# Another order of work in the first 40 microseconds of a fused Mamba and FFN kernel, on all engines

## The reference, cut to what matters

```python
x = x + 0.5 * ffn(layernorm(x))        # quantised weights, LoRA, bias
x = x + attn(layernorm(x))             # rmsnorm, Mamba-2, rmsnorm, gated MLP, both with residuals
x = x + 0.5 * ffn(layernorm(x))

# ffn:  W = (q - zeros) * scales        (groups of 64 inputs share a scale and a zero)
#       y = x @ W.T + (1/16) * (x @ lora_A.T) @ lora_B.T + bias
# mamba2: z, xs, B, C, dt = split(h @ w_in.T); xBC = silu(conv4(xs|B|C) + conv_b)
#         dt = softplus(dt + dt_bias); chunked scan with cumulative decay; y * silu(z); @ w_out.T
```

## Time and profile before

| | us |
|---|---|
| median of 3 runs (lowest to highest) | 752.79 (752.75 to 752.86) |
| the profiled execution, its own time | 752.77 |
| its span in the profile | 751.0 |
| TensorE, VectorE, ScalarE, GpSimd busy | 736.6, 639.3, 455.9, 341.7 |
| mean granted TensorE clock | 0.998 of 2.4 GHz |

### The profile page before, as it was taken

How to read it: one execution, slowest core, us unless ns; L and a number is a source line. 1 busy time by engine, 2 the same in 40 slices (tenths; PEclk the granted TensorE clock), 3 DMA queues, 4 the chain that set the end, 5 groups by cost and what they waited for, 6 DMA issues and landing times.

```text
span 751.0 us, 10693 instructions
## 1 busy us (share of the span) xinstructions
PE 736.6 (98%) x3443; PEld 361.7 (48%) x3443; DVE 639.3 (85%) x1254; ACT 455.9 (61%) x895; POOL 341.7 (46%) x393
## 2 busy tenths in 40 slices
PE   8999999999999999979999999999999999999998
PEld 4454455555555565434444444444444444444444
DVE  7899999889989997868999977977977978767994
ACT  4977888687787776444546456456356456444441
POOL 5731546565443458696423243243242242214574
PEclk9999999999999999999999999999999999999999
DMA  8934645575431233330612735634734733434465
GB/s 300 216 76 86 160 100 118 127 132 103 91 84 43 44 79 94 81 98 1 156 27 49 163 56 97 157 57 84 169 57 84 160 66 71 84 71 80 117 169 141
DMA packets 98886, 77.83 MB, mean 104 GB/s; under 512 B 65616, under 2 KB 73104, under 8 KB 98832
## 3 DMA queue, kind: packets, MB, share of 16 engines
q0 software_dynamic: 17280, 31.46, 23.7%
q1 hardware_dynamic: 78640, 41.09, 21.3%
q10 hardware_dynamic: 2912, 4.61, 2.0%
HBM read 24.94 MB, written 5.54 MB: 41 GB/s over the span
## 4 chain that ended last, share of the span: by engine, by line
PE 71%; DVE 16%; POOL 5%; issue 3%; ACT 3%; DMA 2%; SPq 0%; POOLq 0%; ACTq 0%; DVEq 0%
PE PS L2283 60%; DVE stage L1671 2%; PE PS L2429 1%; DMA x_t<-hb 1%; DVE st L1494 1%; PE PS L2421 1%; PE PS L2387 1%; PE PS L2414 1%; PE PS L2418 1%; PE PS L2397 1%; DVE raw L1671 1%; PE PS L2405 1%; PE PS L2379 1%; PE PS L2525 1%; DVE S L1628 1%
## 5 line engine op out<-in xcount | busy, mean ns | idle before, releaser
L2283 PE MATMUL PS<-h,w_in 128*128 128x512 f16 (+1 forms) x504 | 108.1, 369 | 0.0
L2283 PE MATMUL PS<-h,x_t 128*128 128x512 f16 x408 | 95.5, 383 | 0.0
L784 POOL DMA_DIRECT2D xs<-x x42 | 36.7, 881 | 91.5 <-ACT x L1361 90.7
L2283 PEld LDWEIGHTS PS<-h,w_in 128*128 128x128 f16 x504 | 48.8, 98 | 59.9 <-issue 11.0
L2283 PE MATMUL PS<-n_T,stage 128*128 128x512 f16 x288 | 71.9, 380 | 4.0 <-DVEq L1725 4.0
L1361 ACT ACTIVATE x<-PS,d_d 128x512 f32<-128x512 f32 x59 | 40.2, 682 | 39.1 <-PE PS L2283 36.8
L2283 PEld LDWEIGHTS PS<-h,x_t 128*128 128x128 f16 x408 | 39.7, 99 | 49.4 <-issue 4.5
L584 POOL TENSOR_TENSOR r<-mv,mhalf 128x1 f32<-128x1 f32 (+1 forms) x32 | 29.1, 910 | 50.4 <-DVE mv L1498 36.4
L1331 ACT ACTIVATE xds<-tm,dgh 128x512 f32<-128x512 f32 x24 | 17.3, 722 | 53.1 <-DVE tm L2204 53.1
L2283 PE MATMUL PS<-pre,stage 128*128 128x512 f16 x192 | 49.3, 379 | 0.0
L2283 PEld LDWEIGHTS PS<-n_T,stage 128*128 128x128 f16 x288 | 28.1, 98 | 38.3 <-DVEq L1725 4.5
(11 more groups left out here) (346 smaller groups left out, 1882.8 us busy)
## 6 DMA issues: line engine op xcount, KB each, us to landing
xs<-x POOLq DMA_DIRECT2D x58, 256.0 KB, 3.3
xs<-n POOLq DMA_DIRECT2D x21, 256.0 KB, 3.2
xl<-x POOLq DMA_DIRECT2D x17, 256.0 KB, 3.3
x_t<-x_in SPq DMA_DIRECT2D x16, 256.0 KB, 3.9
x_t<-hb POOLq DMA_DIRECT2D x16, 256.0 KB, 4.4
out<-x_t SPq DMA_DIRECT2D x15, 256.0 KB, 2.3
raw_gu<-gate_t SPq DMA_DIRECT2D x7, 512.0 KB, 4.5
raw_gu<-up_t SPq DMA_DIRECT2D x7, 512.0 KB, 6.4
```

The lines of the kernel that those rows point to most:

```text
L784: po.dma_start(end_row(c), d_tmps[d % 3], accum_op=ALU.add).then_inc(s_acc[d % 3], 16)
L2283: ins = pe.matmul(out_, lhs(a, b, k), rhs(a, b, k), start=first and n == 0, stop=last and n == len(todo) - 1)
```

## The change

No computation is added or taken away. On each engine the calls of the opening stand in another order:

- SP: row 0 is issued first, `lora_b` moves to ScalarE's queue (third there, behind `lora_a` and `zeros`), the bias goes ahead of `q` 2 and 3, and `w_out` is issued after the fourth `t1`.
- GpSimd: `ln0(1)` stands behind the bias scaling and `xb(0)`.
- VectorE: `prep0(0)` ahead of `zero_rows`; `prep0(1)` behind `ffn_weight(1)`, `prep0(2)` behind `ffn_weight(3)`; `ffn_max` behind `x1_stats(0)`; scales and `w_in_lo(0)` ahead of rows 3 and 4. The scaling of the taps becomes a step of its own, `scale_taps`, in the prologue.
- ScalarE: `w_in_sum` earlier, the diagonals later (two groups behind `w_in_hi`, one in the prologue).
- TensorE: transposes and the turns of the maxima stand inside the float32 products, and `conv_taps(b)` waits for its own diagonals only.

```diff
@@ sync
+            load_x(0, 0)
             sp_.dma_start(sc[0:QUAD, :], scales_t).then_inc(s_la, 16)
-            sp_.dma_start(w_rows[QUAD:2 * QUAD, :], lora_b_t).then_inc(s_la, 16)
-            load_x(0, 0)
             load_q(0)
             load_x(1, 1)
             load_q(1)
+            sp_.dma_start(hb[:, :], bias.broadcast_to([P, DM])).then_inc(s_hb, 16)
             load_q(2)
             load_q(3)
-            sp_.dma_start(hb[:, :], bias.broadcast_to([P, DM])).then_inc(s_hb, 16)
...
-            sp_.dma_start(w_out[:, :, :], w_out_t.rearrange("(h p) n -> p h n", p=P)).then_inc(s_wout, 16)
...
             t1(3)
+            sp_.dma_start(w_out[:, :, :], w_out_t.rearrange("(h p) n -> p h n", p=P)).then_inc(s_wout, 16)
@@ gpsimd
-            ln0(1, 1)
             po.wait_ge(s_hb, 16)
             chain(po.tensor_scalar(hb[:, :], hb[:, :], 0.5, None, ALU.mult))
             xb(0, 0)
+            ln0(1, 1)
@@ scalar, prologue
                 hi1(4, 0)
+                build_dw(2)
...
                 hi0(7, 3)
+                ac.wait_ge(e_small, 2)
                 conv(0, 3)
@@ scalar, opening
+            ac.dma_start(sel_rows[QUAD:2 * QUAD, :], lora_a).then_inc(s_la, 16)
             ac.dma_start(zt[0:QUAD, :], zeros_t).then_inc(s_la, 16)
-            ac.dma_start(sel_rows[QUAD:2 * QUAD, :], lora_a).then_inc(s_la, 16)
+            ac.dma_start(w_rows[QUAD:2 * QUAD, :], lora_b_t).then_inc(s_la, 16)
...
             hi0(1, 1)
-            tc0(1)
             ac.wait_ge(s_head, 48)
             ac.activation(a_neg[:, :], al[:, :], ACT.Exp).then_inc(e_aexp, 1)
-            ac.wait_ge(e_tab, 2)
-            build_dw(0)
+            w_in_sum(0)
+            tc0(1)
             hi0(2, 2)
-            build_dw(1)
-            build_dw(2)
+            w_in_sum(1)
             tc0(2)
-            w_in_sum(0)
             hi0(3, 3)
-            w_in_sum(1)
+            w_in_sum(2)
+            hi1(0, 0)
             tc0(3)
-            hi1(0, 0)
-            w_in_sum(2)
             w_in_sum(3)
+            hi0(4, 0)
             hi1(1, 1)
-            hi0(4, 0)
             tc0(4)
             hi1(2, 2)
             hi0(5, 1)
-            hi1(3, 3)
             tc0(5)
             ac.wait_ge(e_scale, 1)
             w_in_hi(W_IN_PIECES[0])
+            hi1(3, 3)
             w_in_hi(W_IN_PIECES[1])
+            build_dw(0)
+            build_dw(1)
@@ vector, small_scales and prologue
-                ve.wait_ge(e_dw, NPC)
-                chain(ve.tensor_scalar(cw[:, :, :], cw[:, :, :], d_ih[:, :], None, ALU.mult))
...
+            def scale_taps():
+                ve.wait_ge(e_dw, NPC)
+                chain(ve.tensor_scalar(cw[:, :, :], cw[:, :, :], d_ih[:, :], None, ALU.mult))
+                ve.sem_inc(e_small, 1)
...
                 lo0(6, 2)
+                scale_taps()
@@ vector, opening
+            prep0(0, 0)
             zero_rows()
-            prep0(0, 0)
             ffn_weight(0)
+            ffn_weight(1)
             prep0(1, 1)
-            ffn_weight(1)
-            prep0(2, 2)
             ffn_weight(2)
             ffn_weight(3)
+            prep0(2, 2)
             prep0(3, 3)
+            x1_stats(0, 0, B_P[0])
             ffn_max()
-            x1_stats(0, 0, B_P[0])
+            x1_stats(1, 1, B_P[1])
             max_row(0)
-            x1_stats(1, 1, B_P[1])
             lo1(0, 0)
             prep0(4, 0)
+            w_in_bound()
             x1_stats(2, 2, B_P[0])
-            w_in_bound()
             lo1(1, 1)
+            max_row(1)
             prep0(5, 1)
-            max_row(1)
+            both_scales()
             x1_stats(3, 3, B_P[1])
-            both_scales()
             lo1(2, 2)
+            w_in_lo(0)
             lo1(3, 3)
             x1_stats(4, 0, B_P[0])
-            w_in_lo(0)
             small_scales()
@@ tensor
             def conv_taps(b):
-                if b == 0:
-                    pe.wait_ge(e_dw, NPC)
+                pe.wait_ge(e_dw, b + 1)
...
+            def first_f(c, k0, k1):
...
+                for k in range(k0, k1):
...
             first_t0(0)
             ffn_parts(2)
             ffn_parts(3)
+            first_f(0, 0, 2)
             first_t0(1)
-            first_f(0)
+            first_f(0, 2, KB)
+            first_f(1, 0, 2)
             first_t0(2)
-            first_f(1)
+            first_f(1, 2, KB)
+            first_f(2, 0, 2)
+            first_t0(3)
             max_turn(0)
-            first_t0(3)
-            first_f(2)
+            first_f(2, 2, KB)
             max_spread(0)
-            first_f(3)
+            first_f(3, 0, 2)
+            first_t0(4)
+            first_f(3, 2, 3)
             max_turn(1)
-            first_t0(4)
+            first_f(3, 3, KB)
+            first_f(4, 0, 1)
             max_spread(1)
-            first_f(4)
+            first_f(4, 1, 2)
             first_t0(5)
-            first_f(5)
+            first_f(4, 2, KB)
+            first_f(5, 0, KB)
```

More of the change, by code:

```diff
@@ L2516, in first_t0 @@
                 last.then_inc(e_n0_tr, 1)
-            def first_f(c):
-                pe.wait_ge(e_n0T, c + 1)
-                if c - 1 > 0:
-                    pe.wait_ge(e_x1, c - 1)
-                for k in range(KB):
+            def first_f(c, k0, k1):
+                if k0 == 0:
+                    pe.wait_ge(e_n0T, c + 1)
+                    if c - 1 > 0:
+                        pe.wait_ge(e_x1, c - 1)
+                for k in range(k0, k1):
                     if c == 0:
@@ L2525, in first_f @@
                     last = pe.matmul(bank(B_P[c % 2]), nT32[c % 2][:, k, :], wf[:, k, :], start=k == 0, stop=k == KB - 1)
-                last.then_inc(e_ffn, 1)
+                if k1 == KB:
+                    last.then_inc(e_ffn, 1)
             def max_turn(n):
```

## The result

The changed kernel takes 756.91 us (median of 6 runs, 756.58 to 757.23), the kernel before it 752.86 on the same chip (6 runs, 752.75 to 753.09): a ratio of 1.0054, 95% interval 1.0041 to 1.0067. That is 3.9 above the forecast of 753.0 and outside both ranges given (751.8 to 754.2, and 750.9 to 755.0 for 8 in 10). The execution profiled here took 756.58 itself, with a span of 754.8.

What follows compares the result with a forecast made beforehand. VectorE's chain was taken as the new bound: the projection's second half moves by +0.1 us and S costs another 0.1, so 752.77 plus 0.2 gives 753.0 us. Own range 751.8 to 754.2; for 8 in 10, 750.9 to 755.0.

Steps and rivals of the forecast that it cites:

- Row 0: VectorE's addition of the bias to row 0 was forecast at 17.1 instead of 19.63, 2.5 us earlier.
- bias landed at 8.7: Bias transfer on SP's queue: landing taken as 8.7 us, between an early bound of 7.7 and a late bound of 9.2.
- `xb(0)` 6.5: Transfer adding the bias to row 0: issued at 10.5, taken as 6.5 us long, landing at 17.0.
- `ffn_max` behind row 0: On VectorE, 3.0 us of `ffn_max` now follow row 0; with 1.8 for row 0, row 1 comes at 21.9.
- after 23: Sign that the forecast is wrong: VectorE adds row 1 before 20.5 or after 23.
- the waits of the fifth and sixth transposes: New TensorE gaps before the fifth and sixth rows' transposes: 0.6 to 1.2 and 0.3 to 0.8, together taken as 1.5 us.
- the fourth row's transpose holding the projection's second half: On TensorE, the projection's second half could start at 41.3 and waits 0.3 us more, until 41.6.
- The sum for TensorE itself: TensorE's opening: start 4.7, plus 32.46 of work, plus 1.5 of gaps, so the first projection starts at 38.7.
- the slow rival: Bias transfers decide: bias at 9.2, `xb(0)` and `xb(1)` taking 7.1 and 7.2, 754.9 us, if `xb(1)` lands after 21.3; chance 0.23.
- The first product: TensorE's first product, behind `lora_b`: forecast at 4.7, bounds 4.2 and 5.2, costing 0.5 us.
- does not do what it says: Rival: queues interleave, row 0 lands at 4.9, first product 5.2, bias unmoved, 753.6 us; chance 0.06, part of "same".
- `ln0(1)` behind the bias: On GpSimd, `ln0(1)` behind the bias scaling makes `hi0(1)` end near 12.5 instead of 11.5, before TensorE's need at 13.9: no cost.

Runs made afterwards that it cites:

- e1: The changed kernel with 12 instead of 7 junk products ahead of TensorE's first real product: 756.81 us.
- e2: The changed kernel with the bias issued third on SP's queue, ahead of all q and of row 1: 755.10 us.
- e3: The changed kernel with both edits, 12 junk products and the bias third on SP's queue: 754.36 us.
- e18: The kernel before with only the taps' diagonals and their scaling late, TensorE's taps waiting for each diagonal by itself: 753.18 us, ratio 0.9996 to 1.0017.
- e17: e13 with ScalarE's `hi1(3)` moved one step further, ahead of the fifth transposed copy `tc0(5)`: 753.86 us.
- e10: e6 with TensorE's opening put back to the order of before, VectorE keeping the changed order: 758.07 us.
- e12: The changed kernel with the early loads, VectorE's opening and TensorE's opening put back as before: 761.68 us.
- e15: e3 with `ffn_max` put back ahead of row 0 on VectorE: 754.42 us.
- e6: The changed kernel with SP's and ScalarE's early loads as before (`w_out` still late) and `zero_rows` ahead of `prep0(0)` on VectorE: 755.71 us.
- e9: e6 with `ffn_max` put back ahead of row 0 on VectorE: 754.24 us.
- e5: The kernel before with the change's order of loads and nothing else of it: 754.99 us.
- e7: The changed kernel with only VectorE's opening put back to the order of before: 758.96 us.
- e14: e9 with row 3's `hi1(3)` and `lo1(3)` moved ahead of the projection's weights on ScalarE and VectorE: 757.33 us.
- e13: e12 with GpSimd's `ln0(1)` ahead of its wait for the bias and ScalarE's `hi1(3)` ahead of the first `w_in` piece: 756.80 us.
- e4: The changed kernel with the early loads of SP and ScalarE in the order of before, `w_out` still late: 756.01 us.

## Why the forecast was wrong, point by point

**Row 0 was the step that failed**, in two of its three terms: bias landed at 8.7 (10.85 measured, +2.15) and `xb(0)` 6.5 (7.63, +1.1); the 1.8 on GpSimd held (1.82). The sum said 17.1, the chip 20.54. That 3.4 is nearly all of the 3.9. Put 17.1 into the relation above and S comes at 17.1 + 69.74 = 86.84, 0.35 later than before, against the 0.2 of the forecast. So all that follows row 0 in the sum was right to some tenths: `ffn_max` behind row 0 (+4.8 to row 1, measured 4.76; row 1 came at 25.30 for 21.9, beyond the sign "after 23"), the waits of the fifth and sixth transposes (0.6 to 1.2 and 0.3 to 0.8; 1.17 and 0.50), the fourth row's transpose holding the projection's second half by 0.3 (0.27). The sum for TensorE itself, 4.7 + 32.46 + 1.5, came out as 5.51 + 34.56 + 1.67. Its 2.1 of longer work is the half rate of the opening, but that is not what made the projection late: e1 ran at the full rate and started it 0.15 earlier.

**The bias's landing** was scaled with its place in SP's queue. Issued 1.42 sooner, with q2 and q3 behind it, it took 1.7 longer and landed later than before; the "late bound" of 9.2 had no room for a longer transfer. In e2, three places earlier, it took 4.3, so the place counts, but not by the bytes ahead of it alone. I had even written the slow rival with the right transfers, the bias at 9.2 and `xb` at 7.1, and gave it 0.23; its sizes were too small (10.85 and 7.63) and with them its 754.9. Its other condition, a late `xb(1)`, did not decide: row 1 had no idle time ahead of it at 25.30.

**The first product** was put at 4.7 with a late bound of 5.2, it came at 5.51: lora_b took 3.7 and not the 2.6 that it had taken at the front of its queue. The rival "does not do what it says" named this interleaving for row 0, which did land early (3.9 forecast; issued at 0.79, taken 3.2). The small inputs paid. The section "Issuing engines are not separate DMA queues" of the page "DMA: Bandwidth & Descriptors" of the Trainium skill fits that: moving lora_b to another engine's queue gave it no path of its own.

**The half rate was not in the forecast at all.** The trace of before had no idle time between junk and first product, so I read the junk as a fixed cost and not as something that sets the rate of what follows. With the start 0.8 late it put the first transposes at 11.55, not at 8.2. By itself it cost nothing (e1), since the bias was later still; once the bias is early it is worth 0.7 (e2 to e3), although lora_b landed 0.7 later in e3's profile. So a bias in time would not have brought row 0 to 17.1 either: TensorE's product held it at 19.18 in e2 and at 18.03 in e3.

**Right as forecast:** the late diagonals cost nothing that could be measured (e18). For the late output weights no run stands alone; e17 bounds them, with the rest that it keeps, by 0.9. **Wrong on GpSimd:** I had costed `ln0(1)` behind the bias at nothing: "`hi0(1)` ends at about 12.5 instead of 11.5, while TensorE needs it at 13.9: nothing". It ended at 15.3 (e10, e12); 1.8 of these 2.8 are the bias, landed at 10.5 there and not at 8.7. The changed order on TensorE covers that, so it did not show in the changed kernel, where VectorE's statistics of row 1 held `ln0(1)` until 14.34; in e10 and e12 it cost 2.3 to 2.4.

Of the 3.79 at S the pair accounts for 2.20 (after to e3; 2.5 in the medians), the place of `ffn_max` for 0.27 on top (e3 to e15, where the medians show nothing; 1.66 where VectorE waits for row 0, e6 to e9), and 1.32 are left in e15. I read this rest as two things: row 3's place behind the scale, and a transpose of the fourth row that took 3.5 us there and 2.7 in the changed kernel. No run removed either alone, and the rest stays argued.

## What to carry to other kernels

A step that fills a wait is free only where it stands. Before moving it behind the thing that is waited for, compute the arrival time at which the new order breaks even (here 16.75 at best, from the 69.74 us behind it), and ask whether every transfer on that path can make it. When an order was changed on several engines at once, undoing one engine's part does not measure this part: it breaks covers that the other engines' orders rely on, and must be read wait by wait.

## What the runs showed of the hardware

**With few warm-up products and an idle time behind them the first real ones run at half rate, and the clock column may not show it.** Idle 1.09 behind seven junk products (after), 1.47 (e2), 1.42 (e5) and 1.73 (e7): the next two pairs took 1.7 to 1.9 each, the third 0.9 to 1.6. Idle 0.17 and 0.85 behind twelve (e1, e3), and none (e15): 0.96 to 0.97 for the first pair and 0.86 from then on. The junk of the changed kernel and of e1, then the first products of e14, which follow seven junk products without idle time:

```profile
1.24 3.17 PE L2511 MATMUL PS<-junk 128*128 128x512 bf16 x7 [1.24 <-DVE junk L1481]
```

```profile
1.24 4.38 PE L2511 MATMUL PS<-junk 128*128 128x512 bf16 x12 [1.24 <-DVE junk L1481]
```

```profile
4.20 1.91 PE L2295 MATMUL PS<-h 128*128 128x512 f32 x2
5.91 1.49 PE L2298 MATMUL PS<-h 128*128 128x512 f32 x2
```

Seven junk products took 0.45 each, the five more of e1 0.24 each (0.33 in e15): the seven ran at the lower rate, and the rate rose behind them. Without idle time behind seven the outcome differs by execution: the first pair took 0.86 in e6 and 1.01 in the kernel before, but 1.7 in e10, e14 and e18. The runs don't separate the number of junk products from the idle time, nor show what makes one execution's rate rise sooner.

In the running kernel waits of 1.09 before and 1.30 (e9) left the rate alone, as did 2.01 (e13) and 2.79 (e14) ahead of the projection; 2.28 (e12), 2.42 (e10), 2.61 (e4), 2.98 (e7) and 3.60 (e12) did not. The length of the idle time alone doesn't decide it. The by-stretch rows (stretch, us, busy times, clock, DMA share, GB/s) of the changed kernel, and then of e10 behind its wait:

```profile
5.50:10.60 5.10, 5.09 (x6) 2.18 (x7) 1.83 (x3) 0.81 (x1) 1.14 (x4) 1.00 0.81 262
```

```profile
15.80:21.00 5.20, 5.20 (x11) 2.14 (x9) 0.62 (x3) 3.32 (x6) 3.21 (x6) 0.67 0.91 214
```

The granted clock beside pairs of 0.86 is 1.00, the level of 2.4 GHz; pairs of 1.7 take twice as long, as at 1.2 GHz. The second stretch has eight matmuls that took 5.30 for 3.60, and the granted clock says 0.67. The first has three pairs spaced 1.86, 1.71 and 1.61, and it says 1.00. The Trainium skill, page "TensorE: Matmul & The Clock Gate", section "Seeing it yourself", warns that the clock's trace events are unreliable on trn2; the trace agrees, 1.00 beside 1.86 for one pair. Where the first instructions matter, read the rate from the spacing of the products.

**The same transfer takes 4.3 to 7.7 us in this opening.** The bias, 256 KB, took 7.0 to 7.7 in the changed order of loads (e5, e1, after, e7), 5.7 to 6.3 in the old one (6.0 before), and 4.3, 5.4 and 4.6 when third (e2, e3, e15): about 1 us of it differs under one and the same order. `xb(0)` took between 6.5 (e17) and 8.1 (e2), and about 5.4 in e5, where it went out at 15.01. In the changed order the DMA engines moved less from 5.5 to 9.0. The changed kernel, then the one before:

```profile
5.50:9.00 3.50, 3.49 (x4) 1.51 (x5) 0.67 (x1) 0.81 (x1) 1.14 (x4) 1.00 0.74 228
```

```profile
5.50:9.00 3.50, 2.44 (x6) 0.76 (x4) 2.87 (x6) 0.81 (x1) 1.24 (x4) 1.00 0.98 360
```

That is 228 GB/s for 360, at a busy share of 0.74 for 0.98. What in the mix of transfers slows them wasn't isolated.
